# Attention tile: the first half of the q projection ahead of the transposes of o

## The reference

```
h = layernorm(x)
q, k, v, beta = h@Wq, normalised(h@Wk), h@Wv, sigmoid(h@Wb)
S_t = S_{t-1} + k_t (beta_t (v_t - k_t^T S_{t-1}))^T ;  o_t = q_t^T S_t
o = o * rsqrt(mean(o*o) + eps) * norm_w * silu(h@Wg)
x = x + o.reshape(b, n, 256) @ Wo
x = x + sum over the two chosen experts of w_e * (gelu(layernorm(x) @ w1[e].T) @ w2[e].T)
```

## Time and profile before

| | before |
|---|---|
| median of 3 runs | 916.29 us (912.56 to 917.0) |
| profiled execution | 911.73 us |
| its span | 909.9 us |
| TensorE busy | 848.1 us (93%) |
| VectorE, ScalarE, GpSimd busy | 626.6, 603.8, 440.7 us |
| mean granted TensorE clock | 0.986 |

### The profile page before, as it was taken

How to read it: one execution, slowest core, us unless ns; L and a number is a source line. 1 busy time by engine, 2 the same in 40 slices (tenths; PEclk the granted TensorE clock), 3 DMA queues, 4 the chain that set the end, 5 groups by cost and what they waited for, 6 DMA issues and landing times.

```text
span 909.9 us, 29758 instructions
## 1 busy us (share of the span) xinstructions
PE 848.1 (93%) x9998; PEld 671.5 (74%) x9999; DVE 626.6 (69%) x1832; ACT 603.8 (66%) x1645; POOL 440.7 (48%) x430
## 2 busy tenths in 40 slices
PE   3789999999999999999987899999999999999995
PEld 2478887788877888777876677777777777777773
DVE  4578898898988988889885675544455554555552
ACT  3488887898888888888876855444446444454551
POOL 2154555677676776766746563322223232323333
PEclk8899999999999999999998999999999999999999
DMA  6022222233332333323232153322233323222223
GB/s 226 2 63 74 84 65 77 84 95 95 95 107 83 95 90 99 103 83 95 78 123 85 55 150 51 54 37 43 43 49 66 53 47 46 46 46 46 47 37 35
DMA packets 50653, 67.16 MB, mean 74 GB/s; under 512 B 6464, under 2 KB 35008, under 8 KB 50528
## 3 DMA queue, kind: packets, MB, share of 16 engines
q1 hardware_dynamic: 36640, 46.46, 17.6%
q0 software_dynamic: 13344, 17.97, 11.5%
q10 hardware_dynamic: 544, 1.05, 0.3%
HBM read 41.84 MB, written 23.61 MB: 72 GB/s over the span
## 4 chain that ended last, share of the span: by engine, by line
PE 63%; POOL 6%; issue 4%; DVE 3%; DMA 3%; ACT 3%; DVEq 0%; POOLq 0%; ACTq 0%
PE ps L1153 59%; DMA wst<-w 3%; PE ps L1527 2%; POOL kscale L616 1%; PE ps L1242 1%; ACT inverse_levels L789 1%; POOL w_lo L665 1%; PE ps L1407 1%; POOL Ll L679 1%; POOL ors L616 1%; POOL w_s L665 1%; POOL routed_rows L694 1%; DVE nL L1750 1%; DVE inverse_levels L1791 1%; POOL out L769 1%
## 5 line engine op out<-in xcount | busy, mean ns | idle before, releaser
L789 ACT ACTIVATE inverse_levels<-ps 128x512 f16<-128x512 f32 (+1 forms) x324 | 169.9, 539 | 166.4 <-PE ps L1527 142.1
L769 POOL DMA_INDIRECT out<-inverse_levels,yidx x71 | 119.1, 1677 | 253.0 <-DVE inverse_levels L2249 183.8
L1153 PE MATMUL ps<-inverse_levels,w_hi 128*128 128x256 f16 (+1 forms) x1376 | 195.8, 254 | 1.6 <-issue 0.8
L1153 PE MATMUL ps<-inverse_levels,w_lo 128*128 128x256 f16 (+1 forms) x688 | 167.3, 253 | 0.0
L2212 DVE SCALAR_TENSOR_TENSOR KpAT<-kq_wvg,inverse_levels 128x512 f16<-128x512 f32 (+1 forms) x144 | 98.4, 688 | 88.7 <-ACT inverse_levels L789 88.7
L1153 PE MATMUL ps<-w_s,inverse_levels 128*128 x426 | 140.5, 379 | 2.9 <-DVE inverse_levels L2249 2.0
L1153 PEld LDWEIGHTS ps<-inverse_levels,w_hi 128*128 x1376 | 122.0, 98 | 14.4 <-issue 2.5
L1153 PE MATMUL ps<-w_s,KpAT 128*128 x426 | 116.1, 273 | 0.0
L1052 ACT ACTIVATE kq_wvg<-ps 128x512 f32<-128x512 f32 (+1 forms) x144 | 85.0, 590 | 41.1 <-PE ps L1153 36.4
L789 ACT ACTIVATE inverse_levels<-kq_wvg 128x512 f16<-128x512 f32 (+1 forms) x144 | 89.8, 623 | 4.6
L616 POOL TENSOR_TENSOR kscale<-karg,fc 128x8 f32<-128x8 f32 x32 | 52.7, 1645 | 82.0 <-DVE karg L1721 82.0
(11 more groups left out here) (239 smaller groups left out, 1919.7 us busy)
## 6 DMA issues: line engine op xcount, KB each, us to landing
wst<-w SPq DMA_DIRECT2D x58, 256.0 KB, 2.9
inverse_levels<-eye SPq DMA_DIRECT2D x35, 256.0 KB, 2.7
x_s<-x SPq DMA_DIRECT2D x32, 128.0 KB, 2.6
out<-x_s SPq DMA_DIRECT2D x32, 128.0 KB, 1.7
x_s<-routed_rows SPq DMA_DIRECT2D x7, 260.0 KB, 2.7
Lh<-routed_rows SPq DMA_DIRECT2D x7, 260.0 KB, 2.8
Vp<-routed_rows SPq DMA_DIRECT2D x7, 260.0 KB
rowA<-routed_rows SPq DMA_DIRECT2D x7, 260.0 KB
```

The costliest lines, as they stand in the source:

```text
L769: pool.indirect_dma_start(out=out, out_offset=bass.IndirectOffsetOnAxis(ap=yidx[:, q, a:a + 1], axis=0), in_=yrow[:, q % 2, a, :], in_offs ...
L789: return act.activation(dst, src, ACT.Copy, scale=scale)
L1153: return pe.matmul(dst, lhsT, rhs, start=start, stop=stop, **kw)
```

## The change

Two calls in TensorE's loop change places. The same instructions are issued with the same waits, on the same data; no other engine's list changes.

```diff
@@ -1489,8 +1489,8 @@
                 k_proj(i - 1, 1)
                 x_make(i - 2, 1)
                 y_make(i - 3, 6)
+                q_proj(i - 1, 0)
                 oT_make(i - 4)
-                q_proj(i - 1, 0)
                 y_make(i - 2, 2)
                 q_proj(i - 1, 1)
                 beta_proj(i - 1)
```

## The result

The changed kernel takes 924.67 us (median of 6 runs, 921.02 to 927.57) against 915.14 us for the kernel before (6 runs, 911.49 to 917.24): a ratio of 1.0108, 95% interval 1.0083 to 1.0134, or 9.5 us more. Forecast were 11.5 us more, for a median of 927.8 us. In the experiments one slow execution of the kernel before (2137.14 us) and one of e8 (931.55 us) are left out of the medians and ratios.

A forecast was written before the change was run, and what follows sets the result against it. It took the path from the transposes over ScalarE and VectorE back to TensorE as the bound; 8 x 0.60 + 12 x 0.43 + 8 x 0.17 + 0.1 = 11.5 us on the 916.3 us median gave 927.8, range 919 to 934.

The forecast's parts named there:

- The path from the transposes: From the transposes of o over ScalarE and VectorE to first_w on TensorE: 4.0 us whatever the wait in front.
- gain rival: Waits before the transposes go and nothing comes back: -5.8 us, 910.5 us; chance 0.04.
- The size per pass: Start of y_make row to first_w: 4.72 us in the new order; later by 0.67 less the wait that goes.
- no wait: 8 passes whose transposes start 0.12 us after the y_make row: first_w 0.60 us later each, 4.8 us.
- short wait: 12 passes with 0.18 us of wait before the transposes: first_w 0.43 us later each, 5.2 us.
- long wait: 8 passes with 0.46 us of wait before the transposes: first_w 0.17 us later each, 1.4 us.
- low clock: The pass at 145 us, where TensorE ran slower and q_proj's second half sets beta_exp: 0.1 us.
- same path, same shift: Passes whose tile starts a sequence, without r_make: y_make(i-2, 3) waits for x_evac behind q_evac, the shift as elsewhere.
- Absorbed: Shift reaches first_w but is mostly taken up before the next pass: half gives 922 us, all about 916; chance 0.13.
- The weight load: fp32 weight load of a transpose behind 56 ns matmuls: taken as 0, bounds 0 to 4.1 us.
- The new wait of beta_proj: TensorE idles some 0.5 us in front of beta_proj, which starts 0.26 us after the end of VectorE's oT_low.
- The clock: More idle per pass makes TensorE's granted clock fall more often: three more stretches, +4.2 us, 932 us; chance 0.07.

The follow-up runs named there:

- e8: Kernel before, with the beta product in its own PSUM bank and ScalarE's state_hi ahead of its copy of the transposes: 917.86 us, ratio 1.0042.
- e7: Changed kernel with both halves of the q projection (24 matmuls) ahead of the transposes of o: 945.35 us, ratio 1.0326 to the kernel before.
- e3: Changed kernel with the beta product in a PSUM bank of its own, so beta_proj no longer waits for oT_low: 924.16 us, ratio 1.0105.
- e10: Kernel before, with beta's own bank, ScalarE's copy of the transposes behind state_hi and k_square, VectorE's oT_low behind y_masked and state_low: 920.12 us.
- e5: Changed kernel with the beta product in its own PSUM bank and ScalarE's state_hi ahead of its copy of the transposes: 918.24 us, ratio 1.0048.
- e2: Kernel before with y_make(i-2, 2) right behind the transposes and both halves of q behind it: 937.60 us, ratio 1.0093.
- e9: Changed kernel with beta's own bank, ScalarE's copy of the transposes behind state_hi and k_square, VectorE's oT_low behind y_masked and state_low: 918.55 us.

## Why the prediction was right

**The path from the transposes.** It was taken to have no time to spare on ScalarE and VectorE, at 4.0 us to first_w whatever the wait in front. Measured 3.92 in the changed kernel, 3.91 with all of q ahead. The gain rival needed over 0.67 us to spare there; the measured distance grew by none of it, and e7's 1.34 us came through whole as well. That q_proj in its old place is beside this path was only just so. TensorE's own order, with both halves of q ahead of beta_proj, was ready at the same time as ScalarE: in the long-wait passes beta_exp starts 0.1 us after the end of beta_proj, and when e8 made ScalarE ready sooner, beta_exp stayed where it was.

**The size per pass.** Forecast were 4.72 us from y_make to first_w in each kind of pass, measured 4.70 (4.42 to 4.48 where a sequence starts). Term by term, against the same pass of the kernel before:

| kind of pass | forecast | measured |
|---|---|---|
| no wait (8) | 8 x 0.60 = 4.8 us | 7 passes 3.9 us, and one that fell in the low clock |
| short wait (12) | 12 x 0.43 = 5.2 | 4.6 |
| long wait (8) | 8 x 0.17 = 1.4 | 1.3 |
| low clock (1) | 0.1 | 0.5 with the one above |
| sum | 11.5 | 10.2 |

About half of the 1.3 us too much, 0.6, lies in the six passes whose tile starts a sequence. The prediction says of them "same path, same shift", and that is the step that does not hold. ScalarE has no state_hi there and reaches beta_exp 1.92 to 1.97 us after the transposes in place of 2.07, right behind beta_proj, which decides there (e3). So their shift is 0.25 to 0.36 us where the wait was short, not 0.43. That they are also 0.12 us shorter from beta_exp to first_w is the same before and after, and cancels. Another 0.2 us is the pass at 58 us, which took 4.27 before and not 4.12.

**Absorbed.** The rest of the passes is 281.3 us before and 281.8 after: nothing was taken up, and half a microsecond came on top. In the profiles first_w of the last of the 29 passes comes 11.0 us later (464.99 to 475.98), 0.3 of it from ahead of the first pass.

**The weight load.** Taken as 0. The transposes start 0.78 to 0.80 us after the y_make row in 28 of 29 passes, which is what 0.12 and 0.67 give. Both loads together take 0.20 us and the first transpose starts 0.05 after the first load. The prediction's check for this was worked out wrongly: 0.12 less four matmuls of 0.029 us is 0.004 and not 0.03, which leaves the lower bound as it is. The rule of the Trainium skill (TensorE: Matmul & The Clock Gate, "Architectural detail: the array is 16× 32×32, not 1× 128×128") that TensorE can pull weight loads ahead of running matmuls agrees with these rows.

**The new wait of beta_proj.** Forecast were some 0.5 us of idle, measured are 0.29 to 0.44. I named it as what is late next. It is there, but e3 shows that in 23 of the 29 passes it is not what costs the time by itself.

**The clock.** This rival was neither needed nor shown. The profiles differ by 4.8 us behind the last of the passes, and the changed kernel's has more time at the lower clock there. Stretches of the kernel before and of the changed one (bounds, length, busy us of PE PEld DVE ACT POOL, PEclk, DMA):

```profile
480.00:530.00 50.00, 41.27 (x381) 32.20 (x381) 33.27 (x125) 35.41 (x79) 32.68 (x34) 0.93 0.29 92
```

```profile
480.00:530.00 50.00, 41.58 (x401) 34.68 (x399) 32.03 (x118) 37.08 (x95) 29.95 (x31) 0.73 0.32 103
```

But from first_w of the last pass to the end, kernels with and without the new order both have it short and long: before 444.9 and e10 448.4 us, e5 444.9 and changed 449.7. The mean granted clock of the executions says the same: 0.974 to 0.985 in the 17 of the kernel before in the first set, 0.974 to 0.986 in the 6 of the changed one. In the attention passes the changed kernel has one stretch at 1.2 GHz (161.6 to 165.0 us), as the kernel before (144.4 to 147.8).

**From the sum to the median.** 11.5 us were carried to the median, 9.5 came. With the measured 10.2 of front and 0.5 of rest it would have been 10.7; the last 1.2 are within the interval (7.6 to 12.3 us), and so are the 11.5. The forecast of 927.8 us is 3.1 above the median of 924.67: 2.0 by the shift, 1.1 because the kernel before had its median at 916.29 in the first 3 runs and at 915.14 in all 6.

## What to carry to other kernels

A wait on the fullest engine is worth what the path through it is worth, and no more. Before filling it with other work, measure from the instruction that waits to the next place where the same engine depends on its result; if that distance is the same in passes with and without the wait, as it was here to about 0.1 us, what is put in front is added in full, less the wait that it fills. Work that stands behind such an instruction and has nobody waiting for it may be in its best place, the more so if it covers another wait there, as q_proj did here (e2).

The chain of waits names one path. Here another one ran beside it with 0.1 us to spare, and each edit alone gave nothing or little in most passes; only both together gave the 0.3 us per pass. When both were cut and more (e9), a third one, over GpSimd, took the gain back.

## What was not expected

The time from a release to the start of the instruction behind it reads like idle: 0.1 us from the end of beta_proj to beta_exp on ScalarE, 0.25 to 0.26 from the end of oT_low to beta_proj, 0.09 from the end of r_make to first_w (314.39 to 314.48 in the chain of waits of the changed kernel). I had counted the first as idle that could be filled; in e8 it was still there.

The waits for weight pieces react to edits that do not touch them. ScalarE waited 4.4 us for them in the kernel before and 11.7 in e8:

```profile
ACT w_s L789 <- DMA wst<-w: 3.6, 7, 0.8
ACT w_hi L789 <- DMA wst<-w: 0.8, 1, 0.8
```

```profile
ACT w_s L789 <- DMA wst<-w: 9.1, 11, 1.8
ACT w_hi L789 <- DMA wst<-w: 2.6, 4, 1.7
```

The first pair is the wait list of the kernel before, the second that of e8, between 58 and 475 us (who waits for whom, us in total, times, longest). Loading 64 of 512 columns gave 6.1 us, more than any order of the instructions that was tried. So the one buffer for all pieces is where I would look next; a second buffer was not tried.
